# A fused four-stage sequence kernel: conditional weights loaded ahead of a packing cut into parts, and derivative products with a rounded operand and its rest

## The chip, the cores and the metric

The kernel runs on one core of one Trainium2 chip. The time is device microseconds (us) of one execution. It was run three times, and once more under the hardware profiler. TensorE is called PE, VectorE DVE, ScalarE ACT, GpSimd POOL and SyncE SP. In this kernel every DMA is issued by SP, in program order.

## The reference

Sixteen samples, each a 256 x 256 float32 matrix `x`, go through four stages one after the other.

```python
# stage 0: adapter, its expert chosen per sample
h = gelu(x @ down_W.T + down_b); h = where(valid, h @ expert_W[i].T + expert_b[i], h) + domain_emb[i]
x = layernorm(h @ up_W.T + up_b + x) * gamma0 + beta0
# stage 1: attention block, 16 heads of 16, with a bias of 16 x 256 x 256 a sample, a mask, and adaptive scale/shift
x1 = ln(x) * (1 + scale) + shift
x2 = x1 + (softmax(q k^T / 4 + bias, mask) v) @ Wo + bo
x3 = x2 + (u * sigmoid(1.702 u)) @ W2 + b2          # u = (ln(x2) * g2 + beta2) @ W1 + b1
# stage 2: one of three small networks, chosen per sample by `condition`
x4 = x3 + net_kind(x3);  f = ln(x4) * gamma + beta
# stage 3: finite differences over rows and columns
df = -(grad_rows(A0 f) + grad_cols(A1 f)) + 0.5 * (grad2_rows(B0 f) + grad2_cols(B1 f) + mixed second derivatives of B2 f)
out = max(f + df * dt, 0)
```

Derivatives along columns are elementwise work on shifted slices. Derivatives along rows are matrix products with two constant 256 x 256 matrices, `d1` (first derivative) and `d2` (second), whose entries are small multiples of 0.5: `d1 @ t_u + d2 @ t_r2`.

## The kernel before

The sixteen samples are software-pipelined. The function `turns` runs an iteration `t`, and in one iteration six samples are in work at different stages: G (two ahead: adapter), F (one ahead: norm, q, k, v), X (attention heads), B (one behind: rest of attention and feed-forward up), T (two behind: feed-forward down, chosen network, elementwise products of the derivatives) and U (three behind: derivative products, output). An iteration has 16 slots, `s = 0..15`, one for each head of X. In each slot the five engines run their own hand-written list of steps, and semaphores tie them together. An engine never leaves its order.

In slot s PE computes the scores of head s (L1095 and, for the mask, L1096), transposes the exponentials of head s-2 (`flip`, L993), and does one or two steps of other samples. DVE adds the bias to the scores of head s (L833) and then does that slot's other work. ACT takes the exponentials (L526) and copies most transposed banks to SBUF (L512).

The places that the change touches:

- SP, slot 0: `stack(X, B, 1)` packs the second half of the heads' q and k: 16 DMAs of 64 KB (L371, L372), which PE needs at slot 8. Slot 1: the chosen network's weights go to `wb` (L402), once `e_ready` of the sample before says that DVE has read the temporaries `t_a` and `t_b`, which lie in the same buffer. PE needs `wb` in slot 5 (L1008). Slots 0, 2, 4, ...: the bias of two heads (`side`, L358), after DVE's `biased` of an earlier head. Slot 3: the `ada` row. Slot 9: `stack(F, X, 0)`, 16 DMAs that PE needs at slot 0 of the next iteration, after `kl_ready`. Slot 11: `wc` and `bcr`.
- PE, slots 2 and 3: `differ(U, 0)` and `differ(U, 1)`, each four float32 products (in the trace each is two MATMUL records, L1062). They wait for `u_ready` and `r2_ready`, which DVE gave in slots 12 and 10 of the iteration before.
- DVE, slot 9: `norm_apply(B)` makes `n3`, which PE transposes in slot 10, then `norm_scale(T)` and `norm_shift(T)` make `fN`. Slot 15: `t_e` is finished (L949, `e_ready`). Slot 1: statistics of F's norm (the last of them L762). Slot 4: L825 adds the derivative products.
- Other products of this kernel already use the short format (`fp32r`, one MATMUL record a product) with operands in two parts: L1031, where `n3h` is the rounded value (a copy by ACT) and `n3l` the rest (a subtraction by DVE).

Of the kernel before, what the change touches and what calls it, by code (L numbers as in the profile page):

```python
# [15 lines left out]
P = 128  # L16
# [42 lines left out]
mixed w1_done u1_ready th_ready ff_ready w2_done x3_ready bcf_ready x3c_ready x3_turned x3T_ready b_done gb_ready c_done x4_ready  # L59
x4_stats x4_aggr x4_var x4_rstd f_scaled f_ready  # L60
ga_ready gb2_ready gc_ready r1_ready r2_ready p_ready u_edge u_cols u_inner u_ready
e_edge e_cols e_inner e_ready d_done w_ready w2s_ready out_ready
""".split()


# [31 lines left out]
def build(nc, d):  # L97

    with ExitStack() as ctx:
# [27 lines left out]
        bo = sb("bo", [P, D])  # L127
        gamma3 = sb("gamma3", [P, D])
        beta3 = sb("beta3", [P, D])
        d1T = sb("d1T", [P, KT, S])  # L130
        d2T = sb("d2T", [P, KT, S])
        grid_a = sb("grid_a", [P, TT, D])
        grid_b = sb("grid_b", [P, TT, D])
        grid_c = sb("grid_c", [P, TT, D])
# [73 lines left out]
        t_p = t_e  # L208
        edge_t = sb("edge_t", [P, 2, TT, 2, 4])
        outN = t_r1  # L210
        switch = sb("switch", [P, 1])
        stats = sb("stats", [P, 4, TT, 6])
        mv = sb("mv", [P, 4, TT, 2])
# [85 lines left out]
        def _(e):  # L299
# [3 lines left out]
            def load_all(pairs, count, done):  # L303
# [41 lines left out]
                (b2r[:, :], d["b2"].partition_broadcast(P)),  # L345
                (gamma3[:, :], d["gamma3"].partition_broadcast(P)),
                (beta3[:, :], d["beta3"].partition_broadcast(P)),
                (d1T[:, :, :], d["d1T"].rearrange("(k p) n -> p k n", p=P)),
                (d2T[:, :, :], d["d2T"].rearrange("(k p) n -> p k n", p=P)),
            ), LOADS, ld_set)  # L350

            e.wait_ge(dve_set, 3)
# [6 lines left out]
                            d["side"][bass.ds(x.i, 1), 2 * c:2 * c + 2].rearrange("b h (t p) k -> p (b h) t k", p=P)  # L359
                            ).then_inc(ld_side[c], 16)  # L360

            def stack(x, prev, m):

                if prev is not None:
                    head(e, scored, prev, HM * m + HM - 1)
                for u in range(2):
                    at = slice(64 * u, 64 * u + 64)
                    for b in range(NBLK):
                        to = slice(64 * u + DH * b, 64 * u + DH * b + DH)
                        q_, k_ = (ql if b >= 2 else qh), (kl if b % 2 == 1 else kh)  # L370
                        e.dma_start(qs[to, HU * m:HU * m + HU, :].bitcast(F32), q_[at, m, :].bitcast(F32)).then_inc(ld_stack[m], 16)  # L371
                        e.dma_start(ks[to, HM * m + u:HM * m + HM:2, :].bitcast(F32), k_[at, m, :].bitcast(F32)).then_inc(ld_stack[m], 16)  # L372

            def body(t):
                G, F, X, B, T, U = phases(t)
                for s in range(SLOTS):
                    if is_step(t, s, -1, 5):
                        e.wait_ge(ready, 2 + SET0)
                    if s == 0 and G and not is_step(t, s, -2, 0):
                        wait(e, ev["xa_ready"], G.p)  # L380
                        e.dma_start(xN[:, :, :], d["x"][bass.ds(G.i, 1)].rearrange("b (t p) n -> p (b t) n", p=P)).then_inc(ld_x, 16)
                        wait(e, ev["wexp_ready"], G.p)
                        dom = e.value_load(ids_ok[0:1, 0, bass.ds(G.i, 1)], min_val=0, max_val=NE - 1)
                        e.dma_start(wexp_raw[:, :], d["expert"][bass.ds(dom, 1)].rearrange("e a n -> (e a) n")).then_inc(ld_exp, 16)
                    if s == 0 and F:
                        wait(e, ev["mask_ready"], F.p)
                        e.dma_start(mask_raw[:, :, :], d["mask"][bass.ds(F.i, 1)].rearrange("b (t p) n -> p (b t) n", p=P)).then_inc(ld_mask, 16)
                        if t == -1:
                            for c in range(3):
                                load_side(F, c)  # L390
                    if s % 2 == 0 and X and (s < 12 or F):

                        c = s // 2
                        head(e, biased, X, 2 * c - 1)
                        if not (t == 0 and s == 0):
                            load_side(X if c < NPAIR - 2 else F, (c + 2) % NPAIR)
                    if s == 0 and X:
                        stack(X, B, 1)
                    if s == 1 and T:
                        kind = e.value_load(ids_ok[0:1, 2, bass.ds(T.i, 1)], min_val=0, max_val=NC2 - 1)  # L400
                        wait(e, ev["e_ready"], T.p)
                        e.dma_start(wb[:, :, :], d["wb"][bass.ds(kind, 2)].rearrange("c (k p) n -> p (c k) n", p=P)).then_inc(ld_kind, 16)  # L402
                    if s == 3 and G:
                        wait(e, ev["x1_ready"], G.p)
                        e.dma_start(ada[:, :, :].rearrange("p a n -> p (a n)"), d["ada_rows"][bass.ds(G.i, 1)].rearrange("b n -> (b n)").partition_broadcast(P)).then_inc(ld_ada, 16)
                    if s == 7 and U:
                        e.wait_ge(ev["out_ready"], U.n)
                        e.dma_start(d["out"][bass.ds(U.i, 1)].rearrange("b (t p) n -> p (b t) n", p=P), outN[:, :, :]).then_inc(stored, 16)
                    if s == 9 and F:
                        e.wait_ge(ev["ql_ready"], F.n)  # L410
                        e.wait_ge(ev["kl_ready"], F.n)
                        stack(F, X, 0)
                    if s == 11 and B:
                        kind = e.value_load(ids_ok[0:1, 2, bass.ds(B.i, 1)], min_val=0, max_val=NC2 - 1)
                        wait(e, ev["c_done"], B.p)
                        e.dma_start(wc[:, :, :], d["wc"][bass.ds(kind, 1)].rearrange("c (k p) n -> p (c k) n", p=P)).then_inc(ld_kind, 16)
                        wait(e, ev["x3c_ready"], B.p)
                        e.dma_start(bcr[:, :], d["bc"][bass.ds(kind, 1)].rearrange("c n -> (c n)").partition_broadcast(P)).then_inc(ld_row, 16)
# [76 lines left out]
        def _(e):  # L495
# [18 lines left out]
            def body(t):  # L514
# [3 lines left out]
                for s in range(SLOTS):  # L518
# [71 lines left out]
                    if s in (11, 12, 13, 14) and B:  # L590
                        j = s - 11
                        quarter(e, "w1_done", B, j)
                        for m in range(2 * j, 2 * j + 2):
                            i = e.activation(ffT[:, m, :], two((bbank, abank)[j % 2])[:, m % 2, :], ACT.Identity, bias=b1c[:, m:m + 1])
                        i.then_inc(ev["u1_ready"], 1)
                    if s == 12 and G:
                        e.wait_ge(ev["expert_done"], G.n)
                        e.activation(g1[:, :], fbank[:, 0:S], ACT.Identity, bias=wexp[:, A:A + 1]).then_inc(ev["g1_ready"], 1)
# [15 lines left out]
        def _(e):  # L614
# [110 lines left out]
            def set_grids():  # L725

                e.tensor_scalar(grid_r1[:, :, :], A0[:, :, :], -1.0, None, ALU.mult)
                e.tensor_scalar(grid_r2[:, :, :], B0[:, :, :], 0.5, None, ALU.mult)  # L730
                e.tensor_scalar(grid_p[:, :, :], B2[:, :, :], 0.5, None, ALU.mult)
# [82 lines left out]
            def body(t):  # L814
                G, F, X, B, T, U = phases(t)
                for s in range(SLOTS):
# [23 lines left out]
                    if s == 1 and F:  # L840
                        e.wait_ge(ev["y_ready"], F.n)
                        norm_stats(F, 1, yN, ev["y_stats"], ev["y_aggr"], ev["y_var"])
                    if s == 2 and T:
                        e.wait_ge(ev["w2_done"], T.n)
                        e.wait_ge(ev["x2b_ready"], T.n)
# [48 lines left out]
                    if s == 8 and B:  # L894
# [2 lines left out]
                        e.tensor_tensor(x2[:, :, :], two(abank), x1res[:, B.par, :, :], ALU.add).then_inc(ev["x2_ready"], 1)  # L897
                        e.wait_ge(ev["x2_ready"], B.n)
                        norm_stats(B, 2, x2, ev["x2_stats"], ev["x2_aggr"], ev["x2_var"])
                    if s == 9 and B:  # L900
                        norm_apply(B, 2, n3, x2, ev["x2_rstd"], ev["n3_ready"])
                    if s == 9 and T:
                        norm_scale(T, 3, x4, gamma3[:, :], ev["x4_rstd"], ev["f_scaled"])
                    if s == 9 and T:
                        norm_shift(T, 3, fN, x4, beta3[:, :], ev["f_scaled"], ev["f_ready"])
                    if s == 10 and B:
# [39 lines left out]
                    if s == 15 and T:  # L946
                        e.wait_ge(ev["gc_ready"], T.n)
                        e.wait_ge(ev["e_inner"], T.n)
                        e.tensor_tensor(t_e[:, :, 1:D - 1], t_e[:, :, 1:D - 1], t_c[:, :, 1:D - 1], ALU.add).then_inc(ev["e_ready"], 1)  # L949
                    if s == H - 1 and X:  # L950
                        head(e, biased, X, H - 1)
                        e.tensor_scalar(nanz[:, :, :], negmax[:, :, :], 2.0, 0.0, ALU.mult, ALU.mult).then_inc(ev["nan_ready"], 1)
# [11 lines left out]
        def _(e):  # L964
# [90 lines left out]
                        i = e.transpose(abank[:, q * S + g * P:q * S + g * P + P], cts[:, 2 * u + g, q * P:q * P + P], ident[:, :])  # L1055
                i.then_inc(done, 1)

            def differ(x, q, between):

                for n, (m, u) in enumerate(((d1T, t_u), (d2T, t_r2))):  # L1060
                    for k in range(KT):
                        i = e.matmul(two(fbank)[:, q, :], m[:, k, q * P:q * P + P], u[:, k, :],  # L1062
                                     start=(n == 0 and k == 0), stop=(n == 1 and k == KT - 1))
                        if q == TT - 1 and n == 1 and k == KT - 1:
                            i.then_inc(ev["d_done"], 1)
                        between(n * KT + k)

            def body(t):
                G, F, X, B, T, U = phases(t)
# [2 lines left out]
                for s in range(SLOTS):  # L1072
# [37 lines left out]
                        four(flip)  # L1110
                    elif s == 2:
                        if U:
                            e.wait_ge(ev["u_ready"], U.n)
                            e.wait_ge(ev["r2_ready"], U.n)
                            if F:
                                e.wait_ge(ev["xa_ready"], F.n)
                            differ(U, 0, no_more)
                            four(flip)
                        else:
                            for n in range(4):  # L1120
# [3 lines left out]
                    elif s == 3:  # L1124
# [1 line left out]
                            e.wait_ge(ev["x3_ready"], T.n)  # L1126
                            turn(bbank, x3, ev["x3_turned"])
                        if U:
                            differ(U, 1, no_more)
                            four(flip)  # L1130
                        else:
                            for n in range(4):
# [189 lines left out]
```

## Time and profile before

| | us |
|---|---|
| runs, median (lowest to highest) of 3 | 980.39 (974.18 to 983.80) |
| profiled execution | 977.65 |
| its span, first to last instruction | 975.70 |
| PE busy | 859.2 |
| DVE busy | 741.7 |
| ACT busy | 608.5 |
| POOL busy | 168.5 |
| mean granted TensorE clock | 0.957 of full speed |

The span is what the trace covers; 1.95 us of the profiled execution lie around it. Busy times overlap between engines. PE's figure includes matmuls whose ends are modelled, so for its pace the distance from one start to the next is what to read.

### The profile page before, as it was taken

What the parts mean: (1) busy time and instruction counts of PE and PEld (TensorE: products, weight loads), DVE (VectorE), ACT (ScalarE), POOL (GpSimd) and SP (SyncE); (2) the same over time, 40 slices, a digit from 0 to 9 for tenths busy, and PEclk for the clock granted to TensorE, in tenths of its full rate; (3) what the DMA queues carried; (4) which work ended last, traced back from release to release, by engine and by line L of the source; (5) the groups of instructions that cost most, each with busy time, mean ns of one, the idle gap of its engine ahead of it and who ended that gap; (6) DMA issues with size and microseconds to landing.
All of it is one profiled execution on the core that took longest, in us unless ns stands there. A gap on an engine that the chain in (4) does not pass through costs nothing.

```text
span 975.7 us, 18459 instructions
## 1 busy us (share of the span) xinstructions
PE 859.2 (88%) x5962; PEld 725.2 (74%) x5962; DVE 741.7 (76%) x2441; ACT 608.5 (62%) x1247; POOL 168.5 (17%) x160
## 2 busy tenths in 40 slices
PE   2475989999989998999999898999989899898884
PEld 0354678887878787887888787878878787787773
DVE  3567767796969797787969697888879597959465
ACT  1133867766768685767668585767677686566320
POOL 2110103021212112030212122030302121201010
PEclk9986999999999999999999999999999899999987
DMA  6623546455554646355544546274556545452100
GB/s 205 195 87 120 167 149 183 138 162 149 162 154 145 173 140 158 99 163 154 166 150 156 151 148 179 92 179 134 161 156 163 148 128 163 133 173 63 50 23 21
DMA packets 147735, 137.57 MB, mean 141 GB/s; under 512 B 19298, under 2 KB 144803, under 8 KB 147636
## 3 DMA queue, kind: packets, MB, share of 16 engines
q1 hardware_dynamic: 147636, 136.33, 47.5%
q8 instruction: 53, 0.87, 0.4%
q14 instruction: 46, 0.38, 0.1%
HBM read 98.49 MB, written 4.23 MB: 105 GB/s over the span
## 4 chain that ended last, share of the span: by engine, by line
PE 33%; DVE 29%; SPq 17%; issue 10%; DMA 7%; ACT 3%; POOL 1%; DVEq 0%; POOLq 0%
SPq L371 7%; SPq L372 6%; DVE sc L833 6%; DMA wb<-in_wb 5%; PE front_bank L1031 4%; PE turn_bank L993 4%; PE back_bank L1008 4%; DVE ffT L925 3%; PE back_bank L1017 3%; PE attend_bank L1017 2%; PE front_bank L1201 2%; DVE pt L958 2%; PE context_bank L1047 2%; PE back_bank L1037 2%; SPq L306 2%
## 5 line engine op out<-in xcount | busy, mean ns | idle before, releaser
L526 ACT ACTIVATE sc<-sc,negmax 128x256 f32<-128x256 f32 x512 | 230.1, 499 | 39.4 <-DVE negmax L833 38.7
L833 DVE CUSTOM_DVE_ANT_0 sc<-score_bank,side 128x256 f32<-128x256 f32 x512 | 195.3, 419 | 56.0 <-PE score_bank L1096 48.2
L512 ACT ACTIVATE pt<-turn_bank 128x512 f32<-128x512 f32 x176 | 104.5, 594 | 160.2 <-PE turn_bank L993 128.9
L993 PE MATMUL turn_bank<-ident,sc 128*128 128x128 f32 x1024 | 160.9, 281 | 1.6 <-ACT sc L526 1.5
L993 PEld LDWEIGHTS turn_bank<-ident,sc 128*128 128x128 f32 x1024 | 127.2, 144 | 36.4 <-issue 14.7
L449 POOL TENSOR_TENSOR rstd<-var,half_neg 128x2 f32<-128x2 f32 x64 | 49.7, 777 | 490.1 <-DVE var L762 488.7
L1095 PE MATMUL score_bank<-ks,qs 128*128 128x256 f32 x512 | 124.0, 324 | 7.3 <-DVE negmax L833 6.5
L1037 PE MATMUL back_bank<-w,ffT 128*128 128x256 f32 x512 | 118.0, 379 | 0.0
L1037 PEld LDWEIGHTS back_bank<-w,ffT 128*128 128x128 f32 x512 | 97.1, 190 | 12.6
L1096 PE MATMUL score_bank<-mask_neg,ident_r 128*128 128x512 f32 x256 | 102.6, 401 | 0.0
L1095 PEld LDWEIGHTS score_bank<-ks,qs 128*128 128x128 f32 x512 | 79.7, 196 | 15.6 <-DVE negmax L833 8.1
L958 DVE COPY pt<-turn_bank 128x512 f32<-128x512 f32 x80 | 54.8, 685 | 46.7 <-PE turn_bank L993 46.6
L1047 PE MATMUL context_bank<-pt,vp 128*18 128x256 f32 x1024 | 68.0, 383 | 5.1 <-ACT pt L512 5.1
L1008 PE MATMUL back_bank<-ctxT,wb 128*128 128x256 f32 x128 | 41.6, 482 | 30.5 <-DMA wb<-in_wb 30.5
L925 DVE SCALAR_TENSOR_TENSOR ffT<-th,ffT 128x512 f32<-128x512 f32 x64 | 56.7, 885 | 3.5 <-ACT th L604 3.5
L1008 PEld LDWEIGHTS back_bank<-ctxT,wb 128*128 128x128 f32 x128 | 29.4, 240 | 39.2 <-issue 34.3
L484 POOL TENSOR_TENSOR x<-x,b2r 128x512 f32<-128x512 f32 x16 | 21.0, 1311 | 179.9 <-DVE xa L935 177.2
L1096 PEld LDWEIGHTS score_bank<-mask_neg,ident_r 128*128 128x128 f32 x256 | 49.3, 193 | 0.0
L1047 PEld LDWEIGHTS context_bank<-pt,vp 128*18 128x18 f32 x1024 | 24.8, 97 | 29.5 <-issue 15.7
L1031 PE MATMUL back_bank<-n3h,w 128*128 128x256 f32 x128 | 38.3, 299 | 7.7 <-DVE n3l L908 7.7
L1062 PE MATMUL front_bank<-t_u,d1T 128*128 128x256 f32 x128 | 34.8, 396 | 8.3 <-DVE t_u L931 8.3
L833 DVE DVE_READ_ACCUMULATOR2_ANT negmax<- 128x1 f32 x512 | 42.0, 82 | 0.0
(199 smaller groups left out, 1939.2 us busy)
## 6 DMA issues: line engine op xcount, KB each, us to landing
side<-in_side SPq DMA_DIRECT2D x128, 512.0 KB, 5.6
qs<-qh SPq DMA_DIRECT2D x128, 64.0 KB, 2.6
ks<-kh SPq DMA_DIRECT2D x128, 64.0 KB, 2.6
ks<-kl SPq DMA_DIRECT2D x128, 64.0 KB, 2.6
qs<-ql SPq DMA_DIRECT2D x128, 64.0 KB, 2.6
wb<-in_wb SPq DMA_DIRECT2D x16, 512.0 KB, 3.9
xN<-in_x SPq DMA_DIRECT2D x16, 256.0 KB, 5.7
ada<-ada_rows SPq DMA_DIRECT2D x16, 256.0 KB, 6.0
```

What stands on the lines that cost most here:

```text
L512: e.activation(pt[:, h % NP2, :, :], two(tbank[h % 2]), ACT.Copy).then_inc(copied[h % 4], 1)
L526: i = e.activation(sc[:, h % NS, q, :], sc[:, h % NS, q, :], ACT.Exp, bias=negmax[:, q, h:h + 1], scale=-1.0)
L833: i = e.tensor_tensor_reduce(sc[:, s % NS, q, :], two(sbank[s % 2])[:, q, :], side[:, (H * X.i + s) % NSIDE, q, :], -1.0, 3.4e38, ALU.add, ...
L925: e.scalar_tensor_tensor(out=f, in0=th[:, j % 2, :, :], scalar=1.0, in1=f, op0=ALU.add, op1=ALU.mult).then_inc(ev["ff_ready"], 1)
L958: e.tensor_copy(pt[:, h % NP2, :, :], two(tbank[h % 2])).then_inc(copied[h % 4], 1)
L993: i = e.transpose(tbank[h % 2][:, k * S + q * P:k * S + q * P + P], sc[:, h % NS, q, k * P:k * P + P], ident[:, :])
L1008: i = e.matmul(two(dst)[:, m, :], w[:, k, c0 + m * P:c0 + m * P + P], xt[:, k, :], start=(k == 0), stop=(k == n_k - 1))
L1031: i = e.matmul(two(dst)[:, m, :], a[:, k, c], b[:, k, :], start=(n == 0), stop=(n == 3 * KT - 1))
L1037: i = e.matmul(two(bbank)[:, q, :], ffT[:, k, q * P:q * P + P], w2[:, k, :], start=(q == 0 and k == 0), stop=(q == TT - 1 and k == FM - 1))
L1047: i = e.matmul(two(cbank)[CG * j:CG * j + VW, g % 2, :], vp[:, x.par, k, QD * g + j, :], pt[:, j, k, :], start=(k == 0), stop=(k == TT - 1))
L1095: e.matmul(two(sbank[s % 2])[:, q, :], qs[:, s // 2, q * P:q * P + P], ks[:, s, :], start=(q == 0), stop=False)
L1096: i = e.matmul(sbank[s % 2][:, :], ident_r[:, :], mask_neg[:, X.par, :, :], start=False, stop=True)
```

## The change

On SP, the load of `wb` moves ahead of `stack(X, B, 1)`, into slot 0, with its wait on `e_ready`. Both packings are cut into four parts of four DMAs, one part in each of slots 0 to 3 and 9 to 12.

In the derivatives, the constant matrices are kept in the short format. They are loaded into `t_u` and `t_r2` and copied once by DVE at set-up. The other operand is cut into a rounded part (`r2_h`, `u_h`: copies by ACT in slots 14 and 15 of T) and the rest (`r2_l` by DVE in slot 15 of T, `u_l` by DVE in slot 1, when the sample is U). `u_l` and `r2_l` lie in the buffers `n3h` and `n3l`. `differ` makes eight short-format products instead of four float32 ones, and PE waits for `r2l_ready` and `ul_ready` before the first. On DVE, `norm_scale(T)` moves ahead of `norm_apply(B)` in slot 9.

```diff
-            def stack(x, prev, m):
+            def stack(x, prev, m, blocks):
...
-                for u in range(2):
-                    at = slice(64 * u, 64 * u + 64)
-                    for b in range(NBLK):
+                for b in blocks:
+                    for u in range(2):
+                        at = slice(64 * u, 64 * u + 64)
...
-                    if s == 0 and X:
-                        stack(X, B, 1)
-                    if s == 1 and T:
+                    if s == 0 and T:
                         kind = e.value_load(ids_ok[0:1, 2, bass.ds(T.i, 1)], min_val=0, max_val=NC2 - 1)
                         wait(e, ev["e_ready"], T.p)
                         e.dma_start(wb[:, :, :], d["wb"][bass.ds(kind, 2)].rearrange("c (k p) n -> p (c k) n", p=P)).then_inc(ld_kind, 16)
+                    if s in (0, 1, 2, 3) and X:
+                        stack(X, B, 1, (s,))
...
-                    if s == 9 and F:
+                    if s in (9, 10, 11, 12) and F:
                         e.wait_ge(ev["ql_ready"], F.n)
                         e.wait_ge(ev["kl_ready"], F.n)
-                        stack(F, X, 0)
+                        stack(F, X, 0, (s - 9,))
...
+                    if s == 14 and T:
+                        e.wait_ge(ev["r2_ready"], T.n)
+                        e.activation(r2_h[:, :, :], t_r2[:, :, :], ACT.Copy).then_inc(ev["r2h_ready"], 1)
+                    if s == 15 and T:
+                        e.wait_ge(ev["u_ready"], T.n)
+                        e.activation(u_h[:, :, :], t_u[:, :, :], ACT.Copy).then_inc(ev["uh_ready"], 1)
...
+                e.tensor_copy(d1T[:, :, :], t_u[:, :, :])
+                e.tensor_copy(d2T[:, :, :], t_r2[:, :, :])
...
+                    if s == 1 and U:
+                        e.wait_ge(ev["uh_ready"], U.n)
+                        e.tensor_tensor(u_l[:, :, :], t_u[:, :, :], u_h[:, :, :].bitcast(F32), ALU.subtract).then_inc(ev["ul_ready"], 1)
...
+                    if s == 9 and T:
+                        norm_scale(T, 3, x4, gamma3[:, :], ev["x4_rstd"], ev["f_scaled"])
                     if s == 9 and B:
                         norm_apply(B, 2, n3, x2, ev["x2_rstd"], ev["n3_ready"])
-                    if s == 9 and T:
-                        norm_scale(T, 3, x4, gamma3[:, :], ev["x4_rstd"], ev["f_scaled"])
...
+                    if s == 15 and T:
+                        e.wait_ge(ev["r2h_ready"], T.n)
+                        e.tensor_tensor(r2_l[:, :, :], t_r2[:, :, :], r2_h[:, :, :].bitcast(F32), ALU.subtract).then_inc(ev["r2l_ready"], 1)
...
-            def differ(x, q, between):
-
-                for n, (m, u) in enumerate(((d1T, t_u), (d2T, t_r2))):
+            def differ(x, q):
+
+                for m, parts in ((d2T, (r2_h, r2_l)), (d1T, (u_h, u_l))):
                     for k in range(KT):
-                        i = e.matmul(two(fbank)[:, q, :], m[:, k, q * P:q * P + P], u[:, k, :],
-                                     start=(n == 0 and k == 0), stop=(n == 1 and k == KT - 1))
...
+                        for n, part in enumerate(parts):
+                            first, last = m is d2T and k == 0 and n == 0, m is d1T and k == KT - 1 and n == 1
+                            i = e.matmul(two(fbank)[:, q, :], m[:, k, q * P:q * P + P], part[:, k, :], start=first, stop=last)
+                if q == TT - 1:
+                    i.then_inc(ev["d_done"], 1)
...
-                            e.wait_ge(ev["u_ready"], U.n)
-                            e.wait_ge(ev["r2_ready"], U.n)
+                            e.wait_ge(ev["r2l_ready"], U.n)
+                            e.wait_ge(ev["ul_ready"], U.n)
```

## Rows read from the trace of the kernel before

**Rows 1.** Waits of PE by cause: engine, line, releaser; total us, times, longest.

```profile
PE back_bank L1008 <- DMA wb<-in_wb: 30.5, 13, 3.3
```

**Rows 2.** The chain of waits in order of time, 477 to 532 us: start, duration, what.

```profile
479.41 0.57 SPq L371
...
490.61 3.84 DMA wb<-in_wb
...
500.29 1.42 PE front_bank L1031 x12
```

**Rows 3.** Timeline of PE, slot 5 (start, us, [idle before]); windows (PE first; clock, DMA, GB/s last).

```profile
493.02 0.39 PE L1096 MATMUL score_bank<-mask_neg,ident_r 128*128 128x512 f32 x1
495.30 3.31 PE L1008 MATMUL back_bank<-ctxT,wb 128*128 128x256 f32 x8 [1.88 <-DMA wb<-in_wb]
...
499.57 0.48 PE L1095 MATMUL score_bank<-ks,qs 128*128 128x256 f32 x2
...
494.00:500.00 6.00, 4.70 (x19) 4.00 (x20) 2.34 (x8) 3.77 (x7) 0.00 (x0) 0.72 1.02 310
```

**Rows 4.** Timeline of PE, the same slot, in the iteration that did not wait.

```profile
873.12 0.39 PE L1096 MATMUL score_bank<-mask_neg,ident_r 128*128 128x512 f32 x1
...
875.96 0.48 PE L1095 MATMUL score_bank<-ks,qs 128*128 128x256 f32 x2
```

**Rows 5.** Timeline of PE, the same slot, first and last of the 13 that waited.

```profile
169.84 0.39 PE L1096 MATMUL score_bank<-mask_neg,ident_r 128*128 128x512 f32 x1
...
175.11 0.48 PE L1095 MATMUL score_bank<-ks,qs 128*128 128x256 f32 x2
...
819.29 0.39 PE L1096 MATMUL score_bank<-mask_neg,ident_r 128*128 128x512 f32 x1
821.28 1.97 PE L1008 MATMUL back_bank<-ctxT,wb 128*128 128x256 f32 x8 [1.61 <-DMA wb<-in_wb]
...
823.88 0.48 PE L1095 MATMUL score_bank<-ks,qs 128*128 128x256 f32 x2
```

**Rows 6.** Timeline of PE, slot 2 of two iterations in a row: the derivative products.

```profile
484.57 1.02 PE L1062 MATMUL front_bank<-t_u,d1T 128*128 128x256 f32 x4
...
486.30 0.60 PE L993 MATMUL turn_bank<-ident,sc 128*128 128x128 f32 x4
...
538.70 1.02 PE L1062 MATMUL front_bank<-t_u,d1T 128*128 128x256 f32 x4
```

**Rows 7.** Timeline of DVE, slots 15 to 3 of one iteration.

```profile
479.50 0.68 DVE L949 TENSOR_TENSOR t_e<-t_e,x 128x508 f32<-128x508 f32 x1
...
484.59 0.17 DVE L762 TENSOR_SCALAR var<-mv 128x2 f32<-128x2 f32 x1
...
488.60 0.42 DVE L833 CUSTOM_DVE_ANT_0 sc<-score_bank,side 128x256 f32<-128x256 f32 x1 [0.74 <-PE score_bank L1096]
```

**Rows 8.** The page's list of DMA issues: engine, form, KB each, us to landing.

```profile
wb<-in_wb SPq DMA_DIRECT2D x16, 512.0 KB, 3.9
```

**Rows 9.** Timeline of ACT, slot 5 and slot 15.

```profile
498.64 0.84 ACT L556 ACTIVATE th<-back_bank,bsel 128x256 f32<-128x256 f32 x2 [2.19 <-PE back_bank L1008]
...
531.44 0.60 ACT L512 ACTIVATE pt<-turn_bank 128x512 f32<-128x512 f32 x1 [1.00 <-PE turn_bank L993]
```

**Rows 10.** Timeline of POOL and DVE where both work at once, slots 2 and 14.

```profile
484.85 0.72 POOL L449 TENSOR_TENSOR rstd<-var,half_neg 128x2 f32<-128x2 f32 x1 [6.93 <-DVE var L762]
...
528.91 1.28 POOL L472 TENSOR_TENSOR x1res<-x,bo 128x512 f32<-128x512 f32 x1
...
528.99 1.75 DVE L925 SCALAR_TENSOR_TENSOR ffT<-th,ffT 128x512 f32<-128x512 f32 x1
```

**Rows 11.** Timeline of DVE and PE around `n3`, slots 9 and 10.

```profile
513.04 0.73 DVE L768 TENSOR_SCALAR n<-x,mv,rstd 128x256 f32<-128x256 f32 x2
...
514.64 0.66 PE L978 MATMUL attend_bank<-ident,n 128*128 128x128 f32 x4
```

**Rows 12.** Timeline of DVE, the last sample's sum with the derivative products.

```profile
970.99 0.69 DVE L825 TENSOR_TENSOR t_e<-front_bank,t_e 128x512 f32<-128x512 f32 x1 [3.20 <-PE front_bank L1062]
```

More of the change, by code:

```diff
@@ L61 @@
 ga_ready gb2_ready gc_ready r1_ready r2_ready p_ready u_edge u_cols u_inner u_ready
-e_edge e_cols e_inner e_ready d_done w_ready w2s_ready out_ready
+uh_ready r2h_ready ul_ready r2l_ready e_edge e_cols e_inner e_ready d_done w_ready w2s_ready out_ready
 """.split()
@@ L129, in build @@
         beta3 = sb("beta3", [P, D])
-        d1T = sb("d1T", [P, KT, S])
-        d2T = sb("d2T", [P, KT, S])
+        d1T = sb("d1T", [P, KT, S], F32R)
+        d2T = sb("d2T", [P, KT, S], F32R)
+        u_h, r2_h = sb("u_h", [P, TT, D], F32R), sb("r2_h", [P, TT, D], F32R)
         grid_a = sb("grid_a", [P, TT, D])
@@ L210, in build @@
         outN = t_r1
+        u_l, r2_l = n3h, n3l
         switch = sb("switch", [P, 1])
@@ L347, in _ @@
                 (beta3[:, :], d["beta3"].partition_broadcast(P)),
-                (d1T[:, :, :], d["d1T"].rearrange("(k p) n -> p k n", p=P)),
-                (d2T[:, :, :], d["d2T"].rearrange("(k p) n -> p k n", p=P)),
+                (t_u[:, :, :], d["d1T"].rearrange("(k p) n -> p k n", p=P)),
+                (t_r2[:, :, :], d["d2T"].rearrange("(k p) n -> p k n", p=P)),
             ), LOADS, ld_set)
@@ L1056, in gather @@
                 i.then_inc(done, 1)
-            def differ(x, q, between):
-                for n, (m, u) in enumerate(((d1T, t_u), (d2T, t_r2))):
+            def differ(x, q):
+                for m, parts in ((d2T, (r2_h, r2_l)), (d1T, (u_h, u_l))):
                     for k in range(KT):
-                        i = e.matmul(two(fbank)[:, q, :], m[:, k, q * P:q * P + P], u[:, k, :],
-                                     start=(n == 0 and k == 0), stop=(n == 1 and k == KT - 1))
-                        if q == TT - 1 and n == 1 and k == KT - 1:
-                            i.then_inc(ev["d_done"], 1)
-                        between(n * KT + k)
+                        for n, part in enumerate(parts):
[3 more added lines that the diff above has]
+                    i.then_inc(ev["d_done"], 1)
             def body(t):
@@ L1112, in body @@
                         if U:
-                            e.wait_ge(ev["u_ready"], U.n)
-                            e.wait_ge(ev["r2_ready"], U.n)
+                            e.wait_ge(ev["r2l_ready"], U.n)
+                            e.wait_ge(ev["ul_ready"], U.n)
                             if F:
                                 e.wait_ge(ev["xa_ready"], F.n)
-                            differ(U, 0, no_more)
+                            differ(U, 0)
                             four(flip)
@@ L1128, in body @@
                         if U:
-                            differ(U, 1, no_more)
+                            differ(U, 1)
                             four(flip)
```

## Prediction

> **What bounds the kernel now.** I read the waits by cause first. PE, the busiest engine, has one large wait: for the DMA into `wb`, 30.5 us in 13 iterations [rows 1]. None of its other waits between 150 and 830 us reaches 0.4 us. Then the chain of waits. It runs through DVE in slots 9 to 14, jumps to SP, goes through all 16 DMA issues of the packing from 479.41, and only then reaches `wb`, issued at 490.61 and on the chain for 3.84 us; then PE has it until slot 9 [rows 2]. So `wb` isn't a slow transfer but one queued 11.2 us late behind the packing.
>
> The wait costs more than its length. From the mask product of head 5 to the scores of head 6, the iteration without a wait takes 875.96 - 873.12 = 2.84 us [rows 4]. The one at 493 takes 499.57 - 493.02 = 6.55, so it loses 3.71, of which 1.88 is the wait and the rest is L1008 itself at 3.31 us [rows 3], where the last of the thirteen, after a wait of 1.61, needs 1.97 [rows 5]. In the first case the granted clock had fallen during the wait, from 2.4 to 1.2 GHz: it is 0.72 of full speed on average over 494 to 500 us [rows 3]. By the same subtraction the first of the thirteen loses 5.27 - 2.84 = 2.43 and the last 4.59 - 2.84 = 1.75 [rows 5]; all thirteen together lose **45.5 us**.
>
> What is left once that is taken off is very regular. From one iteration's derivative products to the next is 538.70 - 484.57 = 54.13 us [rows 6], less 3.71 is 50.42; done for the eleven pairs up to 811 us it gives 50.4 nine times and 50.7 and 50.9 once each. In this period DVE works without a gap from slot 9 to slot 3, where it waits for PE again (0.74 us) [rows 7]. PE and DVE run side by side there, with nothing to spare on either.
>
> **Part 1, `wb` first.** Its new place needs `e_ready`, which is given at 479.50 + 0.68 = 480.2 [rows 7]. With the issue it starts near 481 and at 3.9 us to landing [rows 8] is there by 485. PE asks for it after 493.02 + 0.4 [rows 3], so 8 us are in hand. All 13 losses go: -45.5. What is late next? The activation that PE's L1008 feeds waited 2.19 us for it [rows 9]; it starts that much earlier. The next products on PE then have their inputs by my count of the timeline with 0.7 us or more in hand, and the iteration of rows 4, which runs these slots without any wait (it lacks only F's q, k and v), shows no second wait behind the first.
>
> The packing is queued behind: it now starts 1.5 us later, after the wait for `e_ready`, and in slots 2, 10 and 12 one of its parts stands behind a `side` load that waits for DVE. The distance from the first issue to the `wb` issue [rows 2] is 0.64 us a DMA for 16 and the value load. So the last part of the first half goes at about 489 to 491.6 and has landed by 495.5, if it takes as long as the larger `wb` [rows 8]. ACT, which may not overwrite q before, comes to it after L556, a table load and a pair of exponentials, about 499.5; PE reads the packed half later still. For the second half the last part is issued by 522.5, with 8 us to its use. The `side` loads of slots 2 to 4 and 10 to 12, the `ada` row and `wc` go no later than before, since 16 issues no longer stand in one block ahead of them. I cost all of this at nothing. If a part came too late, every us beyond the 4 in hand would cost a us in each iteration.
>
> **Part 2, the products.** Four float32 products take 486.30 - 484.57 = 1.73 us [rows 6]. Twelve short-format ones took 1.42 in the chain [rows 2], 0.118 each, so eight take 0.95. Each call of `differ` saves 0.78, an iteration 1.56 us. That would be all, if PE didn't have to wait for `ul_ready`.
>
> It does. DVE gets `r2_l` in slot 15 and `u_l` in slot 1. Both are subtractions of 128x512, like L949 at 0.68 [rows 7]; back to back one adds 0.60. DVE ended F's statistics at 484.59 + 0.17 = 484.76 [rows 7], 0.19 us after PE had begun the derivative products, and this distance is 0.17 to 0.19 in all twelve iterations that have it. Since DVE has no gap before, both come on top: `u_l` ends at 484.76 + 0.60 + 0.69 = 486.05, and with about 0.1 for the signal PE starts at 486.15 in place of 484.57. **The new wait is 1.6 us and eats the 1.56.** Queued behind it on PE are the flip of head 0, the context product and the scores of head 3; DVE asks for those at 488.60 less 0.74 [rows 7], so it will be idle no longer than now. Net +0.05 an iteration, 12 times: +0.6. PE ahead of DVE can't win elsewhere, since `u_l` is tied to DVE's unbroken run.
>
> On ACT two copies of 0.60 each are added; it was idle 1.00 us in slot 15 [rows 9], and the copies of slot 14 and 15 stand ahead of nothing that PE wants within 2 us. Nothing. POOL: the power for F's norm starts at 484.85 [rows 10], just after the statistics, when `u_l` is also due. What happens when two such instructions meet is seen at 528.9: POOL's sum starts at 528.91 and runs to 530.19, and DVE's L925, started at 528.99, takes 1.75 instead of 0.69 [rows 10]. DVE's next instruction begins within 0.02 us of the last one, POOL's 0.09 us after it, so DVE should be first and POOL wait; that costs nothing, as DVE wants the power only a slot later. In the other order `u_l` would take 0.7 longer, 12 x 0.7 = 8 us; this is in the range. The Trainium skill, "SBUF — State Buffer", has the rule behind this: DVE and GpSimd share a pair of ports, held for the whole instruction, and the one that starts second blocks, also when the DVE instruction merely has two SBUF inputs. The trace agrees with its 1.75.
>
> The order of `n3`: it was begun at 513.04 and PE's transposes at 514.64 [rows 11]. With a scaling of 0.88 ahead it ends at 513.04 + 0.88 + 0.73 = 514.65, so PE waits 0.0 to 0.1. It is earlier than the wait for `u_l` in the same period and vanishes in it.
>
> **The ends.** Set-up gets two copies, at most 2 x 0.68: +0.7. In the three iterations without F, DVE has waits and no statistics, so the saving of the short format stands: 3 x 1.5 = -4.5. The last sample has `r2_l` and `u_l` in a serial tail of which L825 at 970.99 is the end [rows 12]: +1.4 for the two, some more since `differ` now starts only after `t_e` is ready, less what its products save; between 0 and +4, I take +2.2.
>
> **Sum**, against the profiled execution of 977.65: - 45.5 + 0.6 + 0.7 - 4.5 + 2.2 = 931.2. That execution lies 0.3% below the median 980.39, and the runs spread from 974.18 to 983.80, in my reading since the losses at `wb` differ from one to another (1.5 to 5.9 within this trace). Without them I expect less spread; I say **932**.
>
> **Rivals.**
> - *The new wait lowers PE's clock.* For it: a wait of 1.88 did so [rows 3]. Against: 1.40, 1.61 and 1.62 didn't, the second in [rows 5], nor did 2.72 in one case. With a lowered clock the loss was 1.5 to 2.5 us beyond the wait; 12 x 1.8 = +22, giving 954. Chance 0.12.
> - *Something else is late in slots 5 to 9* when PE comes 3.5 us earlier (ACT's table loads and q stand closest). If half of the 45.5 stays: 954. Chance 0.06.
> - *DVE isn't behind at slot 1*, because a wait moved within its run, and the 1.56 is won: 932 - 19 = 913. Chance 0.06; the constant 0.19 speaks against it.
> - *The short format doesn't do what it says*: eight products at the old pace, in 1.73 again. 12 x 1.56 + 4.5 = +23: 955. L1031 [rows 2] speaks against. 0.03.
> - *Slower: the parts of the packing come too late.* Each part is issued in its slot of SP, behind `side` loads. Against the 4 us in hand, a last part that is 8.5 us late costs 4.5 us in each of 13 iterations: 932 + 13 x 4.5 = 990, and from there on it is slower by over 1%; at 10 us late it is 1010. The waits ahead of it (heads 1 and 3 biased, at some 484 and 490) don't show such a delay. 0.03.
> - *Nothing*, within 1%: `wb` is as late as before, since `e_ready` comes later than its row. 0.02.
>
> **How the numbers follow.** The forecast has 0.68. The clock, the late slots and the format end at 954 to 955; the range takes in 954 and on the low side 920 (half the new wait absent), and leaves out 913, 990 and the upper ends of the others. What a measurement of this kernel can tell from no change is about 1%, 10 us. Faster by over 1% holds for all cases but the last two and part of the mixtures: 0.93; within 1% 0.04; slower 0.03.
>
> **What would show it.** Right: no wait of PE for `wb`; a wait of 12 times 1.4 to 1.7 us at `differ` for DVE's `u_l`; eight products in 0.95 us; period 50.5; DVE without a gap from slot 9 to slot 2. Wrong: a granted clock below 1 after slot 2; PE waiting for ACT or DVE in slots 5 to 9; PE or ACT waiting for the packing.

## Result and profile after

The changed kernel takes 923.0 us (median of 4 runs, 921.39 to 924.69), the kernel before 979.09 (four runs, 974.18 to 983.80): a ratio of 0.943, interval 0.938 to 0.948. It is faster by 5.7%; 932 was forecast, within 920 to 955. The profiled execution took 921.48 us, its span is 919.6.

Waits of PE by cause, changed kernel. None for `wb` is left [rows 1]; the one in the middle that is new stands at the products, 12 times.

```profile
PE front_bank L1081 <- issue: 14.5, 12, 1.2
```

PE's timeline in slot 5, against [rows 3] and [rows 4]. From the mask product of head 5 to the scores of head 6 are 473.44 - 470.69 = 2.75 us, where 6.55 had been; L1025 (L1008 of before) is at its fast pace.

```profile
470.69 0.40 PE L1113 MATMUL score_bank<-mask_neg,ident_r 128*128 128x512 f32 x1
470.93 1.89 PE L1025 MATMUL back_bank<-ctxT,wb 128*128 128x256 f32 x8
...
473.44 0.48 PE L1112 MATMUL score_bank<-ks,qs 128*128 128x256 f32 x2
```

SP's timeline: `wb` goes out at 458.02, before any packing, 12.9 us ahead of L1025; the fourth packing part ends with the issue at 468.59.

```profile
458.02 0.38 SPq L403 DMA_DIRECT2D wb<-in_wb  x1
458.45 0.58 SPq L374 DMA_DIRECT2D qs<-qh  x1
...
468.59 0.60 SPq L375 DMA_DIRECT2D ks<-kl  x1
```

The load no longer lands in 3.9 us. Issued right ahead of the packing, it takes 6.7 us in the median and 8.5 at most (by the DMA figures of its line in this trace); the one issued at 458.02 takes 7.67 and is there 5.2 us before PE asks. The least in hand in any full iteration is 4.4 us, where 8 were forecast.

PE's timeline at the products, against [rows 6]. Eight take 464.76 - 463.74 = 1.02 us, the first of them 0.19 to the next; each call used to take 1.73. What PE did before them ends 1.20 us earlier: the new wait. From the first products to the scores of head 5, a stretch that holds both calls, PE takes 470.37 - 463.74 = 6.63 us, where the kernel before took 492.70 - 484.57 = 8.13. The two calls together save 1.50 us. From one iteration's products to the next are 50.20 us.

```profile
463.74 0.35 PE L1081 MATMUL front_bank<-r_h,d2T 128*128 128x256 f32 x1 [1.20 <-issue]
...
464.76 0.60 PE L1010 MATMUL turn_bank<-ident,sc 128*128 128x128 f32 x4
...
513.94 0.36 PE L1081 MATMUL front_bank<-r_h,d2T 128*128 128x256 f32 x1 [1.21 <-issue]
```

What the wait is for isn't named there; the timelines of DVE and POOL show it. `u_l` (L856, shown as `n3h`) ends at 513.15 + 0.69 = 513.84, and PE starts at 513.94. `r2_l` (L966) stands behind `t_e` and has pushed everything after it by 0.6 us [rows 7]. POOL's power, 0.72 us in [rows 10], takes 1.09: it is the one that gives way, as forecast.

```profile
507.97 0.68 DVE L966 TENSOR_TENSOR n3l<-t_r,r_h 128x512 fp32r<-128x512 f32 x1
...
513.07 0.17 DVE L773 TENSOR_SCALAR var<-mv 128x2 f32<-128x2 f32 x1
513.15 0.69 DVE L856 TENSOR_TENSOR n3h<-t_u,u_h 128x512 fp32r<-128x512 f32 x1
...
513.33 1.09 POOL L452 TENSOR_TENSOR rstd<-var,half_neg 128x2 f32<-128x2 f32 x1 [7.54 <-DVE var L773]
```

The chain that ended last went by a third through PE before; now PE has most of it and SP and DMA hardly any.

```profile
PE 62%; ACT 18%; issue 8%; DVE 6%; SPq 4%; DMA 2%; POOL 1%; POOLq 0%; DVEq 0%; ACTq 0%
```

### The profile page after: what moved, and what is told of

It is laid out like the page before. It is cut to its first block, busy times and chain, and to the rows that moved or that the text cites. A ratio compares the mean times of both kernels' runs of the same rounds, so it can differ in the third digit from the quotient of the medians.

```text
span 919.6 us, 18573 instructions
## 1 busy us (share of the span) xinstructions
PE 812.3 (88%) x5962; PEld 694.2 (75%) x5962; DVE 755.9 (82%) x2475; ACT 621.0 (68%) x1279; POOL 172.8 (19%) x160
## 4 chain that ended last, share of the span: by engine, by line
PE 62%; ACT 18%; issue 8%; DVE 6%; SPq 4%; DMA 2%; POOL 1%; POOLq 0%; DVEq 0%; ACTq 0%
PE back_bank L1054 12%; PE turn_bank L1010 9%; PE context_bank L1064 6%; PE score_bank L1112 5%; PE front_bank L1048 5%; PE score_bank L1113 4%; ACT sc L529 4%; PE front_bank L1081 4%; ACT ffT L597 4%; PE back_bank L1034 3%; PE attend_bank L1034 3%; PE back_bank L1025 3%; PE front_bank L1218 2%; SPq L308 2%; ACT L529 2%
## 5 line engine op out<-in xcount | busy, mean ns | idle before, releaser
L1010 PE MATMUL turn_bank<-ident,sc 128*128 128x128 f32 x1024 | 157.2, 276 | 1.3 <-ACT sc L529 1.2
L1010 PEld LDWEIGHTS turn_bank<-ident,sc 128*128 128x128 f32 x1024 | 123.3, 141 | 32.3 <-issue 13.7
L452 POOL TENSOR_TENSOR rstd<-var,half_neg 128x2 f32<-128x2 f32 x64 | 54.3, 848 | 436.6 <-DVE var L773 435.3
L1081 PE MATMUL front_bank<-r_h,d2T 128*128 128x256 f32 x64 | 19.7, 328 | 27.5 <-issue 14.5
L891 DVE SCALAR_TENSOR_TENSOR ql<-front_bank,cols,qh 128x256 fp32r<-128x256 f32 x32 | 14.0, 480 | 34.1 <-ACT qh L566 34.1
L613 ACT ACTIVATE th<-ffT 128x512 f32<-128x512 f32 x64 | 40.4, 631 | 1.1
```

The source lines that it names most:

```text
L1010: i = e.transpose(tbank[h % 2][:, k * S + q * P:k * S + q * P + P], sc[:, h % NS, q, k * P:k * P + P], ident[:, :])
```

## Experiments

"Period" is the distance between the first products of two iterations with all six samples, read from each trace; there are eleven, and where one number is given they agree within 0.2 us. Line numbers differ by a few from kernel to kernel. The kernel before was run again with each group of experiments: 976.51 us with e1 to e4, 979.13 with e5 to e7, 979.47 with e8 and e9; ratios are to these.

**e1: the loads alone.** The kernel before, with the SP hunks of the change and nothing else.

```diff
-                    if s == 0 and X:
-                        stack(X, B, 1)
-                    if s == 1 and T: ...wb...
+                    if s == 0 and T: ...wb...
+                    if s in (0, 1, 2, 3) and X:
+                        stack(X, B, 1, (s,))
...
-                    if s == 9 and F: ... stack(F, X, 0)
+                    if s in (9, 10, 11, 12) and F: ... stack(F, X, 0, (s - 9,))
```

> The kernel before with only the SP part of the change (wb ahead, packing in parts); derivative products in float32, old norm order. My theory (the wait for wb is the whole gain in the middle, the products are eaten by the wait for u_l): no wait for wb, granted clock 1.00 in the middle, period 50.4 us, about 930 us (926 to 934). Rival (the short format is worth its 1.56 us in each of 16 samples): 25 us above the changed kernel, 946 us, with a period of 51.8.

Measured: 931.85 us (928.92 to 933.57), period 50.33, no wait of PE for `wb`. My theory holds, to 2 us. This alone is 44.7 us against the 976.51 of its own group (ratio 0.955, 0.950 to 0.959), and 46.5 between the two profiled executions, of the 56 of the whole change.

**e2: the products alone.** The changed kernel, with the diff of e1 taken back.

> The changed kernel with the SP part undone: whole packing first, wb in slot 1. My theory: the chain through DVE, the packing and wb is untouched, what PE saves at the products it waits more for wb or u_l; only the iterations at the end gain: 970 to 977 us, wait for wb at least 30 us. Rival (products on the critical path): 979 - 25 = 954 us.

Measured: 972.12 us, ratio 0.995 (0.991 to 0.998). Waits of PE: both the old one and the new one.

```profile
PE back_bank L1025 <- DMA wb<-in_wb: 30.8, 14, 3.3
PE front_bank L1081 <- issue: 14.4, 12, 1.2
```

The float32 products of e1 and the short ones of the next run give the same period, 50.33 and 50.31. So in the middle, with the old order of the norms, the short format gains nothing.

**e3: the old order of the norms.**

```diff
+                        norm_apply(B, 2, n3, x2, ...)
                         norm_scale(T, 3, x4, gamma3[:, :], ...)
-                        norm_apply(B, 2, n3, x2, ...)
```

> The changed kernel with norm_apply(B) ahead of norm_scale(T) in slot 9 again. My theory: the new order fills DVE's wait for the power of x2; in the middle it gives 0.1 us an iteration, at the end (iterations without F, where DVE waits) 2 to 4 us: 925 to 928 us in all, period 50.3. Rival A (the order does nothing): 923. Rival B (the order is what my sum missed, all 10 us): 932.

Measured: 927.06 us (925.87 to 928.74), period 50.31. My theory's 925 to 928 and 50.3. The new order is worth 0.11 us in each full iteration and more at the end: the iteration after the eleven takes 48.37 us with it and 49.39 without, the next 43.22 and 43.48. That is 2.5 us up to there; of the rest of the 4.1 between the medians, the traces show only that the first products stand 2.9 us later in e3, and such starts differ by more than that between kernels that do nearly the same up to there. So 2.5 us are shown for the order, and the rest is not.

**e4: wb ahead, the packing in one block.**

```diff
-                    if s in (0, 1, 2, 3) and X:
-                        stack(X, B, 1, (s,))
+                    if s == 0 and X:
+                        stack(X, B, 1, (0, 1, 2, 3))
...
-                    if s in (9, 10, 11, 12) and F: ... stack(F, X, 0, (s - 9,))
+                    if s == 9 and F: ... stack(F, X, 0, (0, 1, 2, 3))
```

> The changed kernel with wb ahead but each packing as one block of 16 DMAs (slots 0 and 9). My theory: the order alone removes the wait for wb, the side loads had room anyway: 922 to 925 us. Rival (the parts matter: side loads come 10 us later and PE or DVE waits for them): 2 us or more in each of 13 iterations, 948 us or more.

Measured: 923.78 us (920.60 to 925.15), period 50.18.

**e5: the packing in parts, wb behind two of them.**

```diff
-                    if s == 0 and T: ...wb...
                     if s in (0, 1, 2, 3) and X:
                         stack(X, B, 1, (s,))
+                    if s == 1 and T: ...wb...
```

> The changed kernel with the packing in parts but wb in slot 1 again, behind two parts (8 DMAs, 5.1 us). My theory: wb is issued some 5 us later than in the changed kernel, PE asked for it 7.4 us or less after the landing, so it lands just in time or up to 1 us late: 922 to 935 us. Rival (being behind any packing brings the old wait back): 950 us or more.

Measured: 921.79 us (919.60 to 922.32), period 50.20, no wait for `wb`. I had it landing just in time or late, and that was wrong: in the full iterations it has 2.9 us or more in hand, mostly 4. Against the products it is issued 4.9 us later than in the changed kernel (460.79 to 461.63 here, 458.02 to 463.74 there), but it lands in 3.9 us again (median) in place of 6.7. So the earlier place has `wb` ready only 1.1 us earlier in this iteration. With e4: either half of the SP change removes the whole wait. Leaving behind half of the packing is early enough for `wb`; cutting the packing and moving the load are two ways to one end.

They aren't equally safe. From the landing of the last part of the first packing to ACT's `qh`, which has to wait for it, e4 with one block has 5.2 to 6.4 us in hand in the thirteen iterations from the third on, and the changed kernel 0.6 to 5.3. So the parts gain no time (923.78 against 923.00) and take up some of the room, in one iteration nearly all of it.

**e6: u_l in slot 15.**

```diff
                     if s == 15 and T:
                         ...r2_l...
+                        e.wait_ge(ev["uh_ready"], T.n)
+                        e.tensor_tensor(u_l[:, :, :], t_u[:, :, :], u_h..., ALU.subtract).then_inc(ev["ul_ready"], 1)
...
-                    if s == 1 and U: ...u_l...
```

> The changed kernel with u_l made in slot 15, right behind r2_l, in place of slot 1. The same work on DVE, but PE's wait at the products is gone if it is the position of u_l and not DVE's load that makes it. My theory: no wait at the first product, period 50.20 - 1.3 = 48.9, 12 x 1.3 = 16 us less: 907 us. Rival (DVE is the bound, the wait turns up elsewhere): 920 to 923 us.

Measured: 917.90 us (915.52 to 921.63), period 49.8. The wait at the products is gone, as my theory said, but only 0.4 of the 1.3 us came. So neither of the two forecasts gives the number. Timelines of DVE, POOL and PE, in this order:

```profile
465.93 1.91 DVE L794 SCALAR_TENSOR_TENSOR x<-xa,rstd,ada 128x256 f32<-128x256 f32 x2
...
466.26 1.30 POOL L469 TENSOR_TENSOR x<-x,bcr 128x512 f32<-128x512 f32 x1 [1.71 <-PE back_bank L994]
...
469.28 0.63 PE L994 MATMUL front_bank<-ident,x 128*128 128x128 f32 x4 [0.43 <-DVE t_e L836]
```

DVE's last two scalings of `x1` took 1.91 us in place of 0.88, ending just after a POOL sum that began inside them. In the changed kernel this sum starts at 467.60, after DVE is through; it waits for a transpose of PE, and PE now comes sooner. DVE is then late with L836, and PE waits for it.

**e7: u_l made twice.**

```diff
                         e.wait_ge(ev["uh_ready"], U.n)
+                        e.tensor_tensor(u_l[:, :, :], t_u[:, :, :], u_h..., ALU.subtract).then_inc(ev["ul_once"], 1)
+                        e.wait_ge(ev["ul_once"], U.n)
                         e.tensor_tensor(u_l[:, :, :], t_u[:, :, :], u_h..., ALU.subtract).then_inc(ev["ul_ready"], 1)
```

> The changed kernel with the subtraction that makes u_l done twice, one after the other. My theory (PE's wait at the products is tied to DVE's unbroken run): the wait grows by the 0.7 us of the second one, from 1.2 to 1.9, period 50.9, 12 x 0.7 = 8 us more: 931 us. Rival A (DVE has slack there): 923 us. Rival B (a longer wait lowers the granted clock, as waits from 1.88 us on did for wb): a further 1.5 to 2.5 us an iteration, 950 to 960 us.

Measured: 936.54 us (932.71 to 941.13). PE's timeline has the first products of iterations in a row, and the windows view the stretches around two of them (the clock stands third from the end).

```profile
424.61 0.36 PE L1083 MATMUL front_bank<-r_h,d2T 128*128 128x256 f32 x1 [1.93 <-issue]
...
475.55 0.36 PE L1083 MATMUL front_bank<-r_h,d2T 128*128 128x256 f32 x1 [1.93 <-issue]
...
528.00 0.36 PE L1083 MATMUL front_bank<-r_h,d2T 128*128 128x256 f32 x1 [1.93 <-issue]
```

```profile
473.00:479.00 6.00, 4.07 (x29) 2.94 (x31) 5.30 (x16) 1.39 (x3) 1.09 (x1) 0.74 0.99 181
422.00:428.00 6.00, 4.07 (x40) 2.92 (x38) 5.44 (x19) 2.04 (x5) 1.09 (x1) 1.00 0.79 188
```

The wait grew from 1.20 to 1.93, about what one more subtraction lasts, so it is DVE's. Eight periods are 50.9, as my theory had it; three are 52.45 or 52.46. In those the granted clock had fallen (0.74 on average over 473 to 479 us, between the levels of 1.2 and 2.4 GHz) and cost 1.5 us more. Rival B is real for a wait of 1.93, in three periods out of eleven; that is why the time is above the 931 of my theory.

**e8: e6, and POOL's sum behind x1.**

```diff
                         e.wait_ge(ev["x3_turned"], T.n)
+                        if F:
+                            e.wait_ge(ev["x1_ready"], F.n)
                         e.tensor_tensor(x3c[:, :, :], ...)
```

> Run e6 with one more wait: POOL's sum x3c in slot 4 also waits for x1_ready. In e6 PE no longer waits at the products, but the period fell by 0.4 us only; DVE's second scaling of x1 took 1.91 us for its two instructions there, while POOL's sum ran, against 0.88 in the changed kernel. My theory (the two collide since PE gives POOL its input earlier, and DVE is blocked): the pair is back at 0.9, PE's wait for w_ready goes, period 48.9, about 907 us. Rival (DVE's load is the bound whatever the order): 49.8 and 918 us again.

Measured: 909.33 us (905.75 to 912.38), ratio to the kernel before 0.928 (0.922 to 0.934); period 48.87. Timelines of DVE and POOL: they no longer meet.

```profile
464.68 0.88 DVE L796 SCALAR_TENSOR_TENSOR x<-xa,rstd,ada 128x256 f32<-128x256 f32 x2
...
465.73 1.29 POOL L471 TENSOR_TENSOR x<-x,bcr 128x512 f32<-128x512 f32 x1 [2.43 <-DVE x L796]
```

An added wait made the kernel faster by 8.6 us. This version beats both kernels: with it the short format brings about what it saves, 50.33 - 48.87 = 1.46 us an iteration against e1 (the new order of the norms, 0.11 in e3, is in it too).

**e9: the first packing three slots later.**

```diff
-                    if s in (0, 1, 2, 3) and X:
-                        stack(X, B, 1, (s,))
+                    if s in (3, 4, 5, 6) and X:
+                        stack(X, B, 1, (s - 3,))
```

> The changed kernel with the first packing's four parts in slots 3 to 6 in place of 0 to 3. It measures the slower rival of the prediction, in which the last part lands after ACT wants to overwrite q. The last part is then issued behind the side load of slot 6, some 9 us after the start of the products, and lands 2.6 to 4.4 us after its last issue. My theory (some 4 us in hand, behind that every us costs one in each iteration): ACT's qh waits 1 to 2 us, of which a part is hidden by the slack of ql: period 50.5 to 52, 926 to 942 us. Rival (there is far more in hand): 923 us, period 50.20.

Measured: 998.01 us (989.94 to 1001.26), slower than the kernel before by 2.0% (1.4 to 2.6); periods 52.8 to 54.8. The mechanism is mine, the size wasn't (926 to 942 expected): I put the last part at 9 us after the products and it went at 512.14 - 499.11 = 13.0. Timelines of SP, ACT and PE:

```profile
512.14 0.59 SPq L375 DMA_DIRECT2D ks<-kl  x1
...
516.19 0.84 ACT L566 ACTIVATE qh<-front_bank,cols 128x256 fp32r<-128x256 f32 x2 [3.73 <-DMA ks<-kl]
...
517.99 0.38 PE L1048 MATMUL front_bank<-n3h,wk 128*128 128x256 f32 x1 [2.38 <-DVE ql L891]
```

In the changed kernel the last part goes 4.85 us after the products and ACT's `qh` comes 13.24 us after them; here it is 13.03 and 17.08. So 8.18 us later cost ACT 3.84, and 4.34 us didn't reach it. Of these, 3.0 were in hand in that iteration of the changed kernel, where I had said 4; the rest is mostly that the part landed in 3.9 us here and in 5.4 there. The period grew in two steps. In three periods PE's wait for `ql` was 1.62, 1.76 and 1.97 us, the granted clock stayed at 1.00 over the next 6 us, and the period is 2.6 to 2.9 longer than 50.20. In the other eight the wait was 1.94 to 2.75, the clock fell (0.72 on average over 517 to 523 us), and the period is 3.9 to 4.6 longer. By the waits of both kinds about 0.9 us of that is the lowered clock; I hadn't counted it.

## Why the prediction was right, and where it was off

**The 45.5 us at `wb`** were the right term: e1's profiled execution took 931.15 where the one before less this term is 932.15. The term was about 1.2 us too small. I took 2.84 us as the undisturbed stretch, from the one iteration without a wait [rows 4]; the same stretch takes 476.05 - 473.30 = 2.75 in e1, and 2.75 or 2.76 in every iteration of the changed kernel. These 0.09 us are why e1's period is 50.33 and not 50.42. "What is late next?" was answered by nothing, in all runs without the late packing.

**Packing at nothing** came true in every full iteration, but with less room than I had said, and partly by luck. The 4 us in hand assumed that the last part lands in 3.9 us. In the changed kernel it takes 2.9 to 7.8, and ACT's `qh` follows the landing by 0.6 us at the least (the part issued at 518.78 takes 7.8 and lands at 526.6; `qh` starts at 527.18) and by 5.3 at the most. e9's 4.34 holds a faster landing as well. Ahead of the full iterations ACT did wait for a part once, 3.26 us at 130.09, where the kernel before waited 2.01 for PE at that place. The 8 us in hand for `wb` were 4.4 to 6.6 for the same reason: it landed later than in [rows 8]. The slower rival, 990 at 8.5 us late and 1010 at 10, is the place where a wrong part would have turned the sign: 8.2 us late gave 998, where the rival's own rule says 987. The eleven periods grew by 3.8 us on average, less than its 4.2; the profiled execution also reached its first products 17.7 us later and took 9.2 us more behind the eleven periods, both of which the rule left out.

**The new wait that eats the saving** was right in cause (e7) and in effect (50.33 against 50.31). As a size, PE would have begun the products at 512.57, 0.23 us behind the mask product at 512.34 as in the kernel before, and began at 513.94: 1.37 us late; 1.58 was forecast. Of the difference 0.1 is the new order, which gave 0.11 in e3, and the rest that `u_l` starts 0.08 after the last step of the statistics has begun, not after its end. The two calls' saving was 1.50 and not 1.56; the first short product in slot 2 is 0.19 us from the next, not 0.118. With e1's period this adds up: 50.33 - 1.50 + 1.37 = 50.20, where my working, with its +0.05 an iteration, gives 50.46. Without the 0.11 of the order the wait and the saving cancel, as forecast; that they are equal is a coincidence of this kernel.

**The sum was 9.7 us too high** (931.2 against 921.5 in the profiled executions); by place:
- Up to the first products 1.4. The start can't be told from one trace: this point lies between 210.7 and 219.4 us in the traces of the changed kernel and of e4 to e7, whose start is nearly the same work.
- The eleven full periods 3.6: 0.26 each (0.09 in the base, 0.21 in the wait, less 0.06 in the saving, and rounding), and the two that were 50.7 and 50.9 before, which are as all others now.
- The end 4.6, all of it in the first two of its iterations. The step "so the saving of the short format stands: 3 x 1.5" was right about the saving and wrong in taking it for all that changes there. PE's timeline shows what else was to be had. Before, in the first of these iterations, and after:

```profile
843.13 0.36 PE L1031 MATMUL back_bank<-n3h,w 128*128 128x256 f32 x1 [2.76 <-DVE n3l L908]
```

```profile
792.88 0.36 PE L1048 MATMUL back_bank<-n3h,w 128*128 128x256 f32 x1 [1.64 <-DVE n3l L922]
```

This wait got shorter by the new order of the norms (e3 still has 2.75), which I had costed for the delay of `n3` alone and as hidden. And it no longer ends in a lower clock: windows of before and of e3 around it, shown below in this order, have 0.83 and 1.00, with a wait of the same length. What that is worth is seen from the end of this wait to the next products, a stretch in which PE's work is the same in all four kernels: 21.98 us in before and in e1, where the clock fell (0.78 on average over 794 to 800 us in e1), 20.41 in e3 and 20.42 in the changed kernel. In the next iteration it is 20.57 and 20.45 against 18.92 and 18.92. So the clock is 1.5 to 1.6 us in each of two iterations, beside 1.0 and 0.3 of the order.

```profile
840.00:846.00 6.00, 3.24 (x20) 2.95 (x18) 6.00 (x15) 1.59 (x5) 1.02 (x1) 0.83 0.28 99
```

```profile
795.00:801.00 6.00, 3.25 (x26) 2.95 (x25) 6.00 (x16) 2.15 (x6) 0.92 (x1) 1.00 0.68 157
```

Why e3's wait keeps the clock and the same wait in e1 doesn't is open, so this part of the gain can't be put down to a line of the change. PE's busy time in the two windows doesn't tell them apart, 3.24 and 3.25 us.

**The rivals.** A lowered clock after the new wait didn't come at 1.20 us (0 of 12) and did at 1.93 (3 of 11). The working of this rival read the trace before incompletely: waits of 1.87 (at 442.86) and 2.28 (at 172.51) for `wb` didn't lower the clock either, so there the length alone didn't decide. Nor did the clock fall during the wait of 1.88: it is 1.00 over 493.5 to 495.7 and 0.50 over 495.8 to 499, so it fell when PE had been back at work for some 0.45 us. DVE was behind at slot 1, as said; that `u_l` "is tied to DVE's unbroken run" was too strong, since e6 makes it earlier in the same run and the wait goes. What the run then limits is the later L836, and only through the collision with POOL. I had looked for that collision at `u_l`, where DVE comes first and POOL yields. The Trainium skill, "SBUF — State Buffer", "Who interferes with whom", says that a DVE instruction with two SBUF inputs contends with a GpSimd instruction that reads SBUF. The trace of e6 agrees: DVE's pair ends at 467.84, 0.28 us after the sum on POOL. e6 and e8 show the price here: 1.03 us of DVE an iteration, 0.93 of the period.

## What to carry to other kernels

Read a late DMA from the issuing queue: here 512 KB were not slow but stood behind sixteen short issues of 0.64 us, and either moving the load or cutting the block was enough. Before counting what shorter products save, look at which engine their new operands come from: the rest of a split operand, made late in a run without gaps on DVE, cost PE what the format gave, and making it two slots earlier gave it back once POOL's sum was out of the way. Cutting a block of transfers into parts isn't free either: here it gained nothing beside the moved load, and left as little as 0.6 us before ACT would have had to wait. When an engine comes earlier, look for what it now triggers: a sum on POOL moved into a DVE instruction, and one more wait on POOL was worth 8.6 us.

## What the runs showed of the hardware

- A DVE pair with two SBUF inputs took 1.91 us beside a POOL sum that had started in it, and 0.88 without; the POOL power of 0.72 took 1.09 when DVE's subtraction had begun 0.18 us before it.
- Waits of PE of equal length don't lower its clock each time: 1.93 us did in three of eleven periods; in the kernel before 1.88 and 2.76 did, 1.87, 2.28 and 2.72 didn't; 2.75 didn't in e3; 1.20 never did.
- The 512 KB of `wb` landed in 3.9 us (median) where a `side` load was issued next (before, e5), in 6.7 and 7.0 where the packing was (changed kernel, e4), and in 4.7 in e9, whose packing goes three slots later. The 64 KB packing loads took 2.6 us in the median in one block (before, e4) and about 4 in parts between other loads.
- The eleven periods of the changed kernel repeat within 0.02 us (50.19 to 50.21), so that 0.1 us an iteration can be read from one trace, while the whole time of its four runs scatters by 3.3 us, and the first products lie between 210.7 and 219.4 us in the traces of it and of e4 to e7.
